# Four residual blocks on one core: the last residual added by an identity matmul and copied by ACT, and the first normalisation made by GpSimd

## The chip, the cores and the metric

The kernel runs on one core of a Trainium2 chip. The metric is device time in microseconds (us) of one execution; before the change the median of 3 runs is 767.77 us (767.4 to 771.08). Engines are called by the names of the profile: PE (TensorE), DVE (VectorE), ACT (ScalarE), POOL (GpSimd) and SP (SyncE, which here only issues DMAs).

## The reference

The input x has 8 samples of 16 channels of 128 x 128 float32 values. Four residual blocks follow, each on a group normalisation (8 groups of 2 channels) of the current x. Cut to what matters:

```
x = x + conv3x3_reflect(_gn(x), sum_n route[n] * w_experts[n]) + bias   # route = softmax(mean(_gn(x)) @ fc_w.T + fc_b)
x = x + conv3x3_depthwise(abs(_gn(x)), weight)                          # zero padding
x = x + box17x17_mean(_gn(x))                                           # zero padding
x = x + L3(_gn(x))

def L3(v):
    nbr = sum of the 8 neighbours of v                                  # zero padding
    h = elu(w1 @ repeat(nbr, 8, axis=1))                                # 64 hidden channels, per pixel
    h = elu(w2 @ h); h = elu(w3 @ h); h = elu(w4 @ h)
    F = w5 @ h                                                          # 64 channels, meaned by fours, * 0.1
    return 16 channels
```

The change touches the first normalisation (`_gn` ahead of the first convolution) of samples 3 to 7, and the addition of L3's result to x.

## The kernel before, in words

All eight samples stay in SBUF (`xs`), 128 partitions (8 image rows by 16 channels) by 2048 elements a sample, and are updated in place. A sample is worked in four chunks, or quarters, of 512 elements a partition, which is one PSUM bank. The four blocks of a sample are run by all engines, each with its own written-out order of instructions and semaphores between them:

- Block 0: normalised rows go to `y0` with one reflected column at either side; DMAs issued by SP copy shifted rows into the windows `win0`; PE multiplies those with the mixed weights (`conv_taps`, banks `pc`), DVE adds the result to x (`evacuate`).
- Block 1: the same with `y1`, `win1`. ACT makes `y1`.
- Block 2: POOL normalises into `y2` (a multiplication and an addition for each chunk), DVE makes running sums along rows (`box_scan` into `box_sum`), PE adds over rows by `box_mat` (`box_band`).
- Block 3: DVE normalises into `y3` (which lies in `box_sum`), POOL adds neighbours (`near_sums`), SP's DMAs stack them (`stacks`), and then come four layers of 64 channels with ELU. The four banks `pz` hold four groups of rows. For each layer PE fills bank after bank (`layer`), ACT makes a relu of the negative part and an exp, and DVE joins both (`join` in `elu`, line 991). The fifth product, `last_layer`, fills the bank `po`, and DVE adds `po` to x (`output`, line 1011).

After a set-up and a prologue, every engine runs rounds t = 1 to 8 (`rounds`; 2 to 4 are a hardware loop). In round t the ELU layers of sample t-1 are the frame: 16 steps, numbered `at` = 4 x quarter + layer, and around them lie block 2 of sample t, blocks 0 (rest), 1 and 3's preparation of samples t and t+1, and the start of sample t+2. The output of quarter p is made behind the first layer (l = 0) of the next quarter. In round 8 (and the first quarter of round 7) two of the four banks are clipped on DVE instead of being put through a relu on ACT (`clips`).

ACT makes the first normalisation of sample t+2 (`normal0`, line 579) at steps 6 to 9, one chunk a step:

```
if at in (6, 7, 8, 9):
    normal0(t + 2, at - 6)
```

POOL's order in a round is: scales of block 1, mixing the weights of sample t+2 (`mix`, `spread`), clearing the edges of `y3` (`edges3`), scales of block 3, neighbour sums, scales of blocks 0 and 2, and `normal2`. SP's order is: store of sample t-2, windows of block 1, windows of block 0, stacks; in round 1 the load of sample 5 stands between the two windows.

Of the kernel before, what the change touches and what calls it, by code (L numbers as in the profile page):

```python
# [21 lines left out]
Q = 4  # L22
# [53 lines left out]
def build(nc, x, w_experts, conv_bias, fc_w, fc_b, w_depth, w1, w2, w3, w4, w5, con_early, con_channel, con_late, out):  # L76
    with ExitStack() as ctx:
        def sb(name, shape, dtype=F32):
            return ctx.enter_context(nc.sbuf_tensor(name, shape, dtype))
# [4 lines left out]
        def sem(name):  # L84
            return ctx.enter_context(nc.semaphore(name))
# [16 lines left out]
        near_sum = sb("near_sum", [P, K, W])  # L102
        stack = [sb(f"stack{m}", [P, K, W]) for m in range(M)]
        box_mat = sb("box_mat", [P, 3, P])

        u = sb("u", [P, M, CH])
# [70 lines left out]
        y3_written = sem("y3_written")  # L178
        y3_edges = sem("y3_edges")
        y2_scaled = sem("y2_scaled")  # L180
        box_rows = sem("box_rows")
        near_pairs_done = sem("near_pairs_done")
        near_pairs_first = sem("near_pairs_first")
# [199 lines left out]
        def _(sp):  # L383
# [14 lines left out]
            def one(t):  # L398
                if has(t - 2):
                    store(t - 2)  # L400
                if has(t + 1):
                    sp.wait_ge(conv_mm[1], 2 * (t + 1))
                    sp.nop(nofuse=True)
                    windows1(sp, t + 1, range(2), True)
                first = isinstance(t, int) and t == 1
                if first:
                    sp.wait_ge(x_loaded, loaded(4))
                    load(5)
                if has(t + 2):
                    sp.wait_ge(conv_mm[0], 2 * (t + 2))  # L410
                    sp.nop(nofuse=True)
                    windows0(sp, t + 2, range(2), True)
                if has(t):
                    stacks(sp, t, 0)
                    stacks(sp, t, 1)
                if first:
                    sp.wait_ge(x_loaded, loaded(5))
                    load(6)
                    sp.wait_ge(x_loaded, loaded(6))
                    load(7)  # L420
# [27 lines left out]
        def _(pool):  # L448
# [39 lines left out]
            def normal2(i, c):  # L488
# [7 lines left out]
                pool.wait_ge(y2_scaled, Q * i + c + 1 - Q)  # L496
                pool.tensor_tensor(rows, rows, two, ALU.add).then_inc(y2_written, 1)

            def edges3(i):

                pool.wait_ge(conv_mm[2], Q * i + Q)
                pool.nop(nofuse=True)
                for at in (0, W + 1):
                    pool.memset(y3[:, :, at:at + 1], 0.0).then_inc(y3_edges, 1)
# [15 lines left out]
            def one(t):  # L520
                if has(t + 1):
                    scales(t + 1, 1)
                if has(t + 2):
                    mix(t + 2)
                    spread(pool, t + 2)
                if has(t):
                    edges3(t)
                    scales(t, 3)
                    for c in range(Q):
                        near_sums(t, c)  # L530
                if has(t + 3):
                    scales(t + 3, 0)
                if has(t + 1):
                    scales(t + 1, 2)
                    for c in range(Q):
                        normal2(t + 1, c)
# [25 lines left out]
        def _(act):  # L562
# [43 lines left out]
            def elu(j, q, l):  # L606
# [20 lines left out]
                else:  # L627
# [3 lines left out]
                        exp(m - 1)  # L631
                    exp(M - 1)

            def one(t):
                first = isinstance(t, int) and t == 1
                for p in range(4):
                    for l in range(LAYERS):
                        at = 4 * p + l
                        elu(t - 1, p, l)
                        if has(t + 1):  # L640
                            if at - first in (4, 5):
                                normal1(t + 1, at - first - 4)
                        if has(t + 2):
                            if at == 5 + first:
                                softmax_exp(t + 2)
                            if at in (6, 7, 8, 9):
                                normal0(t + 2, at - 6)

            for c in range(Q):
                normal0(0, c)  # L650
# [16 lines left out]
            windows1(act, 1, (1,), False)  # L667
            stacks(act, 0, 1)
            rounds(act, one)

        @block.tensor
        def _(pe):
# [83 lines left out]
                    last.then_inc(z_mm, 1)  # L757

            def last_layer(j, q):
                pe.wait_ge(g_written, zn(j, q, LAYERS - 1, M - 1))  # L760

                for m in range(M):
                    last = pe.matmul(po[32 * m:32 * m + 32, :], w5T[:, :], elus(LAYERS - 1)[:, m, :],  # L763
                                     start=True, stop=True)
                last.then_inc(out_mm, 1)

            def one(t):
# [105 lines left out]
        def _(dve):  # L873
# [134 lines left out]
                if l == LAYERS - 1 and not carried(j, q):  # L1008
                    join(l, 3)

            def output(j, q):
                dve.wait_ge(out_mm, Q * j + q + 1)
                dve.tensor_tensor(sample(j, q), po[:, :], sample(j, q), ALU.add).then_inc(out_evac, 1)

            def box_scan(i, c):

                if c == 0:
# [36 lines left out]
            def one(t):  # L1054
                first = isinstance(t, int) and t == 1
                for p in range(4):
                    for l in range(LAYERS):
                        at = 4 * p + l
                        elu(t - 1, p, l)
                        if l == 0 and part_before(t, p):  # L1060
                            output(*part_before(t, p))
                        if has(t + 1):
                            if first and at < 2:
                                evacuate(t + 1, 0, at)
# [97 lines left out]
            for d, side in enumerate(("above", "own", "below")):  # L1162
                last = dve.tensor_copy(box_mat[:, d, :], const(f"box_{side}"))
            last.then_inc(matrices, 1)
            evacuate_pair(0, 0, 0)
            stats_of(0, 1, (0, 2))
            evacuate_pair(0, 0, 1)
# [47 lines left out]
            merge_stats(1, 2)  # L1215
            group_var(1, 2)
            rounds(dve, one)
            output(B - 1, Q - 1)

SETUP_DVE = 6 + 9
# [23 lines left out]
```

## Time and profile before

| | before |
|---|---|
| median of 3 runs | 767.77 us |
| lowest, highest | 767.4, 771.08 us |
| the profiled execution | 776.6 us, span 774.7 us |
| mean granted TensorE clock | 0.945 |
| PE, DVE, ACT, POOL busy | 624.3, 611.5, 563.9, 200.6 us |
| PE weight loads busy | 188.2 us |
| DMA | 85.53 MB in 72865 packets |

The span runs from the first to the last instruction of the profiled execution. Busy time counts the time in which at least one instruction of an engine is in work; instructions of one engine overlap, so that the distance of two starts is often shorter than the duration of one.
### The profile page before, as it was taken

What the parts mean: (1) busy time and instruction counts of PE and PEld (TensorE: products, weight loads), DVE (VectorE), ACT (ScalarE), POOL (GpSimd) and SP (SyncE); (2) the same over time, 40 slices, a digit from 0 to 9 for tenths busy, and PEclk for the clock granted to TensorE, in tenths of its full rate; (3) what the DMA queues carried; (4) which work ended last, traced back from release to release, by engine and by line L of the source; (5) the groups of instructions that cost most, each with busy time, mean ns of one, the idle gap of its engine ahead of it and who ended that gap; (6) DMA issues with size and microseconds to landing.
All of it is one profiled execution on the core that took longest, in us unless ns stands there. A gap on an engine that the chain in (4) does not pass through costs nothing.

```text
span 774.7 us, 13144 instructions
## 1 busy us (share of the span) xinstructions
PE 624.3 (81%) x4142; PEld 188.2 (24%) x4142; DVE 611.5 (79%) x1100; ACT 563.9 (73%) x1081; POOL 200.6 (26%) x291
## 2 busy tenths in 40 slices
PE   0351845899798999899889988999899789889992
PEld 0211211223222222233223322322232223222220
DVE  1352785598959998989988998879887889769993
ACT  0112110689868998899889988998898968898882
POOL 1302024402541235213521353125300630230000
PEclk9985886899989999999999999999999999999996
DMA  5759499407985739254834574455640560065002
GB/s 98 139 91 178 101 189 211 73 14 146 170 192 97 173 88 206 66 112 107 183 87 109 110 164 107 109 112 132 141 109 3 125 146 1 2 146 125 1 1 54
DMA packets 72865, 85.53 MB, mean 110 GB/s; under 512 B 8674, under 2 KB 58354, under 8 KB 72818
## 3 DMA queue, kind: packets, MB, share of 16 engines
q1 hardware_dynamic: 68096, 78.58, 47.6%
q10 hardware_dynamic: 4722, 6.34, 4.5%
q8 instruction: 26, 0.43, 0.2%
q14 instruction: 21, 0.17, 0.1%
HBM read 9.14 MB, written 8.39 MB: 23 GB/s over the span
## 4 chain that ended last, share of the span: by engine, by line
PE 36%; DVE 22%; ACT 17%; DMA 8%; issue 8%; SPq 6%; POOL 1%; ACTq 1%; DVEq 0%; POOLq 0%
PE pz L756 19%; PE pc L702 8%; ACT u L610 7%; DVE g L991 6%; ACT u L618 6%; PE pc L733 6%; DMA win<-y 5%; DVE u L987 3%; ACT u L615 2%; DVE bn L923 2%; DVE box_sum L1024 2%; DMA xs<-in_x_dram 2%; DVE xs L974 2%; PE po L763 2%; DMA stack<-near_sum 2%
## 5 line engine op out<-in xcount | busy, mean ns | idle before, releaser
L610 ACT ACTIVATE u<-pz 128x512 f32<-128x512 f32 x472 | 275.4, 603 | 93.3 <-PE pz L756 92.7
L756 PE MATMUL pz<-g,wT 64*64 64x512 f32 x1536 | 296.7, 614 | 18.7 <-DVE g L991 15.1
L991 DVE SCALAR_TENSOR_TENSOR g<-u,pz 128x512 f32<-128x512 f32 x384 | 250.3, 681 | 62.1 <-ACT u L618 58.7
L618 ACT ACTIVATE u<-u 128x512 f32<-128x512 f32 x472 | 289.6, 643 | 1.3
L756 PEld LDWEIGHTS pz<-g,wT 64*64 64x64 f32 x1536 | 80.5, 132 | 212.2 <-issue 210.4
L733 PE MATMUL pc<-win,t 64*32 64x512 f32 x1392 | 98.0, 667 | 27.0 <-DMA win<-y 16.0
L702 PE MATMUL pc<-box_sum,box_mat 128*128 128x512 f32 x180 | 90.9, 621 | 12.3 <-DVE box_sum L1024 12.3
L923 DVE BATCH_NORM_STATS2 bn<-xs 128x6 f32<-128x512 f32 (+1 forms) x128 | 82.8, 682 | 22.0 <-DMA xs<-in_x_dram 20.2
L468 POOL TENSOR_TENSOR stat<-stat,con 128x1 f32<-128x1 f32 x32 | 22.5, 704 | 272.9 <-DVE stat L943 272.9
L991 DVE SCALAR_TENSOR_TENSOR g_last<-u,pz 128x512 f32<-128x512 f32 x128 | 82.5, 680 | 9.1 <-ACT u L618 7.1
L756 PE MATMUL pz<-stack,wT 64*64 64x512 f32 x512 | 81.7, 620 | 9.5 <-DMA stack<-near_sum 4.2
L678 PE MATMUL psm<-stat,con 128*128 128x2 f32 x64 | 12.8, 270 | 56.9 <-DVE stat L931 53.6
L598 ACT ACTIVATE y<-xs,stat 128x1024 f32<-128x1024 f32 (+1 forms) x16 | 19.9, 1258 | 43.7 <-POOL stat L471 43.7
L702 PEld LDWEIGHTS pc<-box_sum,box_mat 128*128 128x128 f32 x180 | 29.9, 188 | 72.7 <-issue 46.1
L733 PEld LDWEIGHTS pc<-win,t 64*32 64x32 f32 x1392 | 24.2, 114 | 93.2 <-issue 93.2
L1024 DVE TENSOR_TENSOR_SCAN box_sum<-y 128x580 f32<-128x580 f32 x32 | 43.1, 1355 | 1.4 <-DMA stack<-near_sum 1.4
L514 POOL TENSOR_TENSOR near_sum<-box_sum 128x512 f32<-128x512 f32 x30 | 31.8, 1059 | 39.5 <-DVE box_sum L1031 39.5
L584 ACT ACTIVATE y<-xs,stat 128x512 f32<-128x512 f32 (+1 forms) x32 | 26.3, 839 | 19.2 <-POOL stat L471 10.1
L518 POOL TENSOR_TENSOR near_sum<-near_sum,box_sum 128x512 f32<-128x512 f32 x30 | 37.7, 1258 | 4.3 <-DVE near_sum L1052 2.0
L756 PEld LDWEIGHTS pz<-stack,wT 64*64 64x64 f32 x512 | 23.5, 134 | 60.3 <-issue 58.1
L763 PE MATMUL po<-g_last,w5T 128*32 128x512 f32 x256 | 35.0, 619 | 2.8 <-DVE g_last L991 2.8
L615 ACT ACTIVATE u<-u 128x512 f32<-128x512 f32 x40 | 25.2, 629 | 12.2 <-DVE u L987 12.2
(87 smaller groups left out, 366.6 us busy)
## 6 DMA issues: line engine op xcount, KB each, us to landing
stack<-near_sum SPq DMA_DIRECT2D x90, 192.0 KB, 4.0
win<-y SPq DMA_DIRECT2D x56, 260.0 KB, 4.2
win<-y SPq DMA_DIRECT2D x56, 195.0 KB, 4.3
out_dram<-xs SPq DMA_DIRECT2D x8, 1024.0 KB
stack<-box_sum SPq DMA_DIRECT2D x60, 128.0 KB, 3.8
xs<-in_x_dram SPq DMA_DIRECT2D x7, 1024.0 KB
stack<-near_sum SPq DMA_DIRECT2D x30, 128.0 KB, 3.4
win<-y ACTq DMA_DIRECT2D x8, 260.0 KB, 8.2
```

The costliest lines, as they stand in the source:

```text
L514: pool.tensor_tensor(o, y[:, :, 0:W], y[:, :, 1:W + 1], ALU.add).then_inc(near_pairs_done, 1)
L518: pool.tensor_tensor(o, o, y[:, :, 2:W + 2], ALU.add).then_inc(near_rows, 1)
L610: act.activation(u[:, m, :], pz[:, m, :], ACT.Relu, scale=-1.0, bias=0.0).then_inc(relu_done, 1)
L615: act.activation(u[:, m, :], u[:, m, :], ACT.Exp).then_inc(exp_done, 1)
L618: act.activation(u[:, m, :], u[:, m, :], ACT.Exp, scale=-1.0).then_inc(exp_done, 1)
L702: mm = pe.matmul(chunk_bank(i, c), box_mat[:, d, :], box_sum[:, c * KB + d:(c + 1) * KB + d, RAD:RAD + W], start=d == 0, stop=d == 2)
L733: last = pe.matmul(pair_banks(i, k, n)[2 * C * m:2 * C * m + 2 * C, h, :], mat[rows, kw, :], blocks(win[m // 2], n + 2 * h)[rows, :, kw:kw ...
L756: last = pe.matmul(pz[to, m, :], wT[rows, l, rows], src, start=True, stop=True)
L763: last = pe.matmul(po[32 * m:32 * m + 32, :], w5T[:, :], elus(LAYERS - 1)[:, m, :], start=True, stop=True)
L923: dve.bn_stats(bn[k][:, c, :], sample(i, c)).then_inc(stat_step[k], 1)
L991: dve.scalar_tensor_tensor(out=elus(l)[:, m, :], in0=u[:, m, :], scalar=-1.0, in1=pz[:, m, :], op0=ALU.add, op1=ALU.max).then_inc(g_writte ...
L1024: dve.tensor_tensor_scan(own_rows(box_sum, c).rearrange("p k w -> p (k w)"), y2[:, c * n + BOX:(c + 1) * n + BOX], y2[:, c * n:(c + 1) * n ...
```

## The change

Three things are altered.

- `last_layer` first multiplies the chunk of x itself with a 128 x 128 identity (`same`, copied from the constants once by DVE) into `po`, and the four products with `w5T` are then added in the bank. ACT copies the bank over the chunk of x; DVE's addition is gone. PE's identity matmul waits for ACT's previous copy.
- `normal0` of samples 3 to 7 goes from ACT's steps 6 to 9 to POOL, ahead of `mix`, as a multiplication and an addition for each chunk and two column copies for each pair of chunks; POOL waits first for all four scans of sample t (`box_rows`). Samples 0 to 2 stay with ACT in the prologue.
- On SP, in round 1, the load of sample 5 stands behind the windows of block 0 instead of ahead of them.

```diff
@@ sync, one(t)
-                if first:
-                    sp.wait_ge(x_loaded, loaded(4))
-                    load(5)
                 if has(t + 2):
                     sp.wait_ge(conv_mm[0], 2 * (t + 2))
                     sp.nop(nofuse=True)
                     windows0(sp, t + 2, range(2), True)
+                if first:
+                    sp.wait_ge(x_loaded, loaded(4))
+                    load(5)
@@ gpsimd
+            def normal0(i, c):
+
+                if c == 0:
+                    pool.wait_ge(norm_step[0], i * NORM + NORM)
+                    pool.wait_ge(win0_in, WIN0 * i)
+                rows = blocks(y0, c)[:, :, 1:W + 1]
+                one, two = (st[0][:, n:n + 1].unsqueeze(2).to_broadcast([P, KB, W]) for n in range(2))
+                pool.tensor_tensor(rows, sample(i, c).rearrange("p (k w) -> p k w", w=W), one, ALU.mult).then_inc(y0_scaled, 1)
+                pool.wait_ge(y0_scaled, Q * i + c + 1 - 3 * Q)
+                pool.tensor_tensor(rows, rows, two, ALU.add).then_inc(y0_written, 1)
+                if c % 2:
+                    half = slice((c - 1) * KB, (c + 1) * KB)
+                    pool.wait_ge(y0_written, Y0 * i + 2 * c)
+                    pool.nop(nofuse=True)
+                    pool.tensor_copy(y0[:, half, 0:1], y0[:, half, 2:3]).then_inc(y0_written, 1)
+                    pool.tensor_copy(y0[:, half, W + 1:W + 2], y0[:, half, W - 1:W]).then_inc(y0_written, 1)
...
                 if has(t + 2):
+                    pool.wait_ge(box_rows, Q * t + Q)
+                    for c in range(Q):
+                        normal0(t + 2, c)
                     mix(t + 2)
@@ scalar
+            def output(j, q):
+                act.wait_ge(out_mm, Q * j + q + 1)
+                act.copy(sample(j, q), po[:, :]).then_inc(out_evac, 1)
...
                         elu(t - 1, p, l)
+                        if l == 0 and part_before(t, p):
+                            output(*part_before(t, p))
...
-                            if at in (6, 7, 8, 9):
-                                normal0(t + 2, at - 6)
@@ tensor
             def last_layer(j, q):
+                if isinstance(j, int) and j == 0 and q == 0:
+                    pe.wait_ge(matrices, 2)
+                else:
+                    pe.wait_ge(out_evac, Q * j + q)
+                pe.nop(nofuse=True)
+                pe.matmul(po[:, :], same[:, :], sample(j, q), start=True, stop=False)
                 pe.wait_ge(g_written, zn(j, q, LAYERS - 1, M - 1))
-
+                pe.nop(nofuse=True)
                 for m in range(M):
                     last = pe.matmul(po[32 * m:32 * m + 32, :], w5T[:, :], elus(LAYERS - 1)[:, m, :],
-                                     start=True, stop=True)
+                                     start=False, stop=True)
@@ vector
-            def output(j, q):
-                dve.wait_ge(out_mm, Q * j + q + 1)
-                dve.tensor_tensor(sample(j, q), po[:, :], sample(j, q), ALU.add).then_inc(out_evac, 1)
...
-                        if l == 0 and part_before(t, p):
-                            output(*part_before(t, p))
...
+            dve.tensor_copy(same[:, :], const("ident")).then_inc(matrices, 1)
```

In DVE's and ACT's lists the output behind the last round goes from one to the other as well.

POOL in the loop of rounds 2 to 4, from the scales of block 1 on, before (`wmix` are the mixed weights, `stat` the statistics and scales):

```order
L468 TENSOR_TENSOR stat<-stat,con 128x1
L469 REGISTER_ALU
L471 TENSOR_SCALAR stat<-stat 128x1
L477 ISA
L479 TENSOR_SCALAR wmix<-wc,route 128x144
```

The same place of the changed kernel, down to the first mixing (`y` is `y0` here, `xs` the samples):

```order
L473 TENSOR_SCALAR stat<-stat 128x1
L543 ISA
L504 ISA
L505 REGISTER_ALU
L508 ISA
L508 TENSOR_TENSOR y<-xs,stat 128x4x128
L509 ISA
L510 TENSOR_TENSOR y<-y,stat 128x4x128
L508 ISA
L508 TENSOR_TENSOR y<-xs,stat 128x4x128
L509 REGISTER_ALU
L510 TENSOR_TENSOR y<-y,stat 128x4x128
```

Two chunks and two column copies, and the same again, now stand between POOL's scales of block 1 and its mixing; L543 is the wait for the scans.

PE around a quarter's first layer in the loop, before (`po` is the output bank, `stack` the layer's input, L702 a box band, L756 the layers):

```order
L756 MATMUL pz<-stack,wT 64x512 x2
L763 MATMUL po<-g_last,w5T 32x512 x4
L702 MATMUL pc<-box_sum,box_mat 128x512
L752 REGISTER_ALU
L756 MATMUL pz<-g,wT 64x512 x2
```

The same place of the changed kernel (L783 are the layers, L792 the identity, L796 the last layer, L729 the band):

```order
L783 MATMUL pz<-stack,wT 64x512 x2
L790 REGISTER_ALU
L792 ISA
L792 MATMUL po<-xs,same 128x512
L796 MATMUL po<-g_last,w5T 32x512 x4
L729 MATMUL pc<-box_sum,box_mat 128x512
L779 REGISTER_ALU
L783 MATMUL pz<-g,wT 64x512 x2
```

One 128 x 128 by 512 matmul, with a wait and a register for its address, has come between the first layer of a quarter and the second.

## Rows read from the trace of the kernel before

**Rows 1.** Windows of rounds 4, 6 and 8: busy us of each engine.
```profile
core 0: us, PE busy (x) PEld busy (x) DVE busy (x) ACT busy (x) POOL busy (x), PEclk, DMA share, GB/s
386.70:466.00 79.30, 73.23 (x520) 22.24 (x516) 72.22 (x129) 71.52 (x140) 26.15 (x37) 1.00 0.55 120
...
544.70:620.10 75.40, 67.79 (x432) 20.27 (x426) 64.73 (x110) 68.40 (x131) 20.34 (x24) 1.00 0.40 91
...
695.30:760.30 65.00, 59.29 (x282) 13.40 (x274) 61.68 (x99) 56.17 (x96) 0.00 (x0) 1.00 0.19 43
```

**Rows 2.** Waits over the span: engine, line, awaited, us, times, longest.
```profile
ACT u L610 <- PE pz L756: 92.7, 54, 32.9
```

**Rows 3.** Timeline of ACT, round 6: start, us, instruction, idle before.
```profile
574.43 1.12 ACT L610 ACTIVATE u<-pz 128x512 f32<-128x512 f32 x2
...
578.45 1.20 ACT L610 ACTIVATE u<-pz 128x512 f32<-128x512 f32 x2
...
583.60 1.08 ACT L610 ACTIVATE u<-pz 128x512 f32<-128x512 f32 x2 [0.90 <-PE pz L756]
```

**Rows 4.** Timeline of PE, round 6, the same steps.
```profile
580.55 1.99 PE L702 MATMUL pc<-box_sum,box_mat 128*128 128x512 f32 x4
582.48 2.31 PE L756 MATMUL pz<-stack,wT 64*64 64x512 f32 x16
584.72 1.06 PE L763 MATMUL po<-g_last,w5T 128*32 128x512 f32 x8
585.72 1.13 PE L702 MATMUL pc<-box_sum,box_mat 128*128 128x512 f32 x2
586.78 1.95 PE L756 MATMUL pz<-g,wT 64*64 64x512 f32 x10
```

**Rows 5.** Timelines of SP, PE and ACT in round 1; the last is round 3.
```profile
182.62 0.71 SPq L385 DMA_DIRECT2D xs<-in_x_dram  x1
183.44 10.46 SPq L339 DMA_DIRECT2D win<-y  x5
...
199.23 1.23 SPq L347 DMA_DIRECT2D win<-y  x2
...
212.45 3.67 PE L733 MATMUL pc<-win,t 64*32 64x512 f32 x32 [3.98 <-DMA win<-y]
...
218.07 1.09 ACT L610 ACTIVATE u<-pz 128x512 f32<-128x512 f32 x2 [7.37 <-PE pz L756]
...
376.60 1.09 ACT L610 ACTIVATE u<-pz 128x512 f32<-128x512 f32 x2 [1.43 <-PE pz L756]
```

**Rows 6.** Timelines of DVE (the last scan) and POOL in round 4.
```profile
416.73 1.36 DVE L1024 TENSOR_TENSOR_SCAN box_sum<-y 128x580 f32<-128x580 f32 x1
...
423.92 0.65 POOL L479 TENSOR_SCALAR wmix<-wc,route 128x144 f32<-128x144 f32 x1 [15.51 <-DVE route L963]
...
437.02 0.57 POOL L468 TENSOR_TENSOR stat<-stat,con 128x1 f32<-128x1 f32 x1 [7.09 <-DVE stat L943]
```

**Rows 7.** POOL's normal2: one line's durations (min, median, max), and a group.
```profile
L495 POOL TENSOR_TENSOR y<-xs,stat x28: 1039/1042/1043, 136.1 to 624.1; 128x512 f32<-128x512 f32 x28
...
L497 POOL TENSOR_TENSOR y<-y,stat 128x512 f32<-128x512 f32 x28 | 29.3, 1045 | 2.2
```

**Rows 8.** Timeline of ACT in round 4, the first normalised chunk.
```profile
420.66 0.88 ACT L584 ACTIVATE y<-xs,stat 128x512 f32 x1
421.36 1.15 ACT L610 ACTIVATE u<-pz 128x512 f32<-128x512 f32 x2
```

**Rows 9.** Timelines of PE and DVE in round 8, and PE's end.
```profile
713.32 1.06 PE L763 MATMUL po<-g_last,w5T 128*32 128x512 f32 x8
714.32 2.25 PE L756 MATMUL pz<-g,wT 64*64 64x512 f32 x12
...
715.26 0.68 DVE L1013 TENSOR_TENSOR xs<-po,xs 128x512 f32<-128x512 f32 x1
715.86 0.68 DVE L991 SCALAR_TENSOR_TENSOR g<-u,pz 128x512 f32<-128x512 f32 x1
...
761.05 1.94 PE L763 MATMUL po<-g_last,w5T 128*32 128x512 f32 x8 [2.80 <-DVE g_last L991]
```

More of the change, by code:

```diff
@@ L104, in build @@
         box_mat = sb("box_mat", [P, 3, P])
+        same = sb("same", [P, P])
         u = sb("u", [P, M, CH])
@@ L180, in build @@
         y2_scaled = sem("y2_scaled")
+        y0_scaled = sem("y0_scaled")
         box_rows = sem("box_rows")
@@ L669, in _ @@
             rounds(act, one)
+            output(B - 1, Q - 1)
         @block.tensor
@@ L1217, in _ @@
             rounds(dve, one)
-            output(B - 1, Q - 1)
 SETUP_DVE = 6 + 9
```

## The prediction

> **What bounds the kernel now.** I read first the busy table cut by round, then the waits, and then the steps of single rounds on ACT, PE and DVE. A round is sixteen steps (four quarters of four layers). In round 4, a middle one, no engine is full: PE is busy 73.2 of 79.3 us, DVE 72.2, ACT 71.5, POOL 26.2 [rows 1]. ACT's relu waits for PE 54 times, 92.7 us in all, the longest 32.9 ahead of round 1 [rows 2]. So a round is a chain that goes through ACT, DVE and PE in turn, and two rules give the start of the next step:
>
> - ACT's rule: a bare step lasts 4.0 us (574.43 to 578.45, eight activations 0.5 apart) [rows 3], and everything else ACT runs is added.
> - PE's rule: the last join of a step lets PE finish the fourth bank of the next layer; then PE does what it has been given behind that layer, and only then the first bank of the layer after it, which ACT's first relu waits for. So a step's start is tied to the start two steps earlier. In round 6, where ACT has no normalisation to make, two such starts lie 583.60 - 574.43 = 9.17 apart with two box bands in between that hold PE from 580.55 to 582.48, 1.93 us [rows 3, 4]. So two steps take at least 7.24 us plus what PE has behind the middle layer; ACT alone needs 8.0 for two. PE can hide 0.76 us per layer, and more where ACT is given other work.
>
> Carried through the sixteen steps of a middle round with DVE's joins 0.60 apart, these rules give 79.4 us for the 79.3 of [rows 1], so I trust them for differences.
>
> **The stall of round 1.** At step 13 ACT stands for 7.37 us; the same place in round 3 has 1.43 [rows 5]. PE waited there for window DMAs (3.98 us) and its next 32 matmuls took 3.67 us. The cause is on SP: the load of sample 5 (1 MB) went out at 182.62, and the first five window copies behind it took 10.46 us to issue; the last pair went out at 199.23 [rows 5]. The change puts these copies ahead of the load. POOL writes y0 earlier than ACT did: it starts behind the last scan, which in round 4 ends at 416.73 + 1.36 = 418.09 [rows 6]; four chunks of 1.042 + 1.045 = 2.09 us [rows 7] make 8.4, with edges and semaphores some 9.3, done at about 427.4, whereas ACT only starts its first chunk at 420.66 and does one per step [rows 8]. So the fourteen copies can go out from 182.6 at some 0.7 us each (1.23 for the last two) and end near 192.5, eight us before the last pair of today; the stall falls to the usual one: 7.37 - 1.43 = **5.9 us gained**. Bounds: nothing gained (the load now runs into the stack copies that follow) and 7.4.
>
> **What POOL pays.** The mix and spread of the same sample, which start at 423.92 today, start at about 427.5 and end some 5.5 us later with the edge memsets, 433; the next thing POOL is waited for is the scale at 437.02, before which it sits 7.09 us [rows 6]. Four us of cover stay, so I price it at nothing; without the cover each us late would be a us on the third scale and the stacks behind it. The added wait on box_rows also holds back those memsets, but nothing that is due earlier than 437.
>
> One doubt is whether POOL's eight instructions and DVE hold each other up. Of POOL's 28 multiplications of the other normalisation, made beside DVE's joins, additions and statistics, the shortest takes 1039 and the longest 1043 ns [rows 7], so they don't; normal0 will run beside the same kinds of DVE work, since the scans are over by then.
>
> **The steps with l = 0.** Four times a round PE gets an identity matmul, ACT a copy, and DVE loses an addition.
> - Identity: 128x128 weights and 512 columns, the shape of one box band. The single band behind the last layer occupies PE from 585.72 to 586.78, 1.06 us [rows 4]. Half of the pair of bands is 0.97. I take 1.06; the ends are 0.5, if part of it falls into PE's own gaps, and 2.0, if its weights or its register address can't be prepared under the layer before.
> - Copy: 0.50, an eighth of a bare step, which is what a relu from such a bank costs [rows 3]; the ends are 0.40 and the 0.70 (420.66 to 421.36) that a normalised chunk takes [rows 8].
> - Addition gone: DVE's own pitch, 715.26 to 715.86, 0.60 [rows 9].
> - normal0 gone from ACT in rounds 1 to 5: 0.70 and, with edges, about 1.1, twice each, 3.6 us a round [rows 8]. What this is worth is seen in round 6, which has none: ACT then waits 0.90 for PE at the very next step [rows 3]. Most of the 3.6 turns into waiting for PE.
>
> Behind an l = 0 layer PE has the last layer (1.00: 584.72 to 585.72) and a band or tap (1.06) [rows 4]: the two-step minimum is 7.24 + 2.06 = 9.30 today and 10.36 with the identity. Carried through a middle round: first quarter +0.4 (the step behind the identity starts 0.9 later, the DVE addition gives 0.5 back, and the rest delays the scans that PE waits for); second -0.2 (ACT bound: +0.5 copy, -0.7 normal0); third +0.1 (+0.9, normal0 gone); fourth -0.4 (+0.8, but two convolution taps that wait for evacuations on DVE start 0.6 earlier each). Sum -0.1: **-0.4 for rounds 2 to 5**.
>
> Round 6 (75.4 us) has no normal0 to lose and round 7 no convolutions [rows 1]: there the identity and the copy are only partly absorbed by the next step's wait, by the same rules **+0.9 each**.
>
> Round 8 (65.0 us, 4.06 a step [rows 1]) is another chain: two banks are clipped on DVE, and clip, exp and join follow one another on DVE and ACT. The next layer starts on PE at 714.32, exactly when the last layer (from 713.32) lets it [rows 9], and it sets the next relu. The identity moves that by 1.06; DVE's addition, 0.60 ahead of the next step's join, gives some 0.4 back, and 0.2 of the rest is free on ACT. That leaves 0.45 a quarter, four times: **+1.8**, with ends 0 (all in gaps) and 4.2 (nothing given back).
>
> At the end the identity lies in PE's wait of 2.80 us for the last join [rows 9], and ACT's copy replaces DVE's 0.68 us addition: nothing. Behind that wait the eight passes of the last layer take 1.94 us against 1.06 in round 6 [rows 4, 9]. The Trainium skill (TensorE: Matmul & The Clock Gate, What's actually happening) says that the array's clock is cut to half when it has been idle and released by activity. By that rule an identity inside the wait could keep the clock up and the last layer be 0.9 shorter, and the sum below would be -3.6; the trace alone gives nothing, since PE still stands for some 1.7 us, and the sum goes by that. The extra DVE copy of the identity (128x128) comes once, in the set-up, where DVE waits for the first convolution: nothing, at most 0.2.
>
> **Sum.** -5.9 - 0.4 + 0.9 + 0.9 + 1.8 = -2.7 against the profiled execution, 776.6 us (span 774.7). That run is 1.1% above the median of 767.77, so I scale: 773.9 / 776.6 x 767.77 = **765.1 us**, 0.35% faster.
>
> **Rivals.**
> - ACT was the bound after all, and all its saving shows. Rounds 1 to 5 then gain 3.6 - 4 x 0.5 = 1.6 each, 8.0, rounds 6 and 7 lose 2.0 each for the copies, round 8 gains the 1.6 of DVE, beside the stall's 5.9: 11.5 us, 756.4. For it: ACT's steps 4 to 9 have no idle time in round 4. Against: the 0.90 of round 6 [rows 3]. Chance 0.12.
> - The stall moves: the load, now behind the windows, is still on the queues when the stack copies of sample 1 are issued, and the first layer of round 2 waits for those. Then the 5.9 is lost: +3.2, 770.9. For it: the load kept SP's queue slow for 10.46 us [rows 5], and the stack copies are the next on that queue. Chance 0.12.
> - Slower: the identity costs about 2.0 us instead of 1.06, since its moving operand comes from an address in a register and its full-width weights may not load under the layer before. Its place is behind every l = 0 layer, where PE's rule is the later one; each 0.1 above 1.06 costs by the rules 0.3 to 0.4 a round over seven rounds. At 1.2 the gain is gone; at 2.0 the total is about +19, 786.6. Against: bands of the same shape stand at 1.06 and their banks and rows vary too. Chance 0.10, of it 0.03 with a cost so small above 1.2 that it can't be told from no change.
> - The forecast: chance 0.66, its own range 761.5 to 768.5.
>
> **How the numbers follow.** About 0.5% (3.8 us) is what a measurement of this kernel can tell from no change, so faster is below 763.9 and slower above 771.6. The forecast gives 0.22 faster and 0.44 same; the first rival 0.12 faster; the moved stall 0.07 same and 0.05 slower; the dear identity 0.03 same and 0.07 slower. That is faster 0.34, same 0.54, slower 0.12. The range 760.0 to 770.8 holds the forecast whole, most of the moved stall and a cheap identity (0.5 instead of 1.06, some 5 us less).
>
> **What would show it.** Right: in round 1 PE has no DMA wait near step 13, and SP's five copies issue in about 4 us; the round is near 82 us; rounds 2 to 5 stay within 0.5 us of 79.3; rounds 6 and 7 grow by about 1 and round 8 by about 2; ACT's waits for PE come behind l = 0 layers. Wrong: an identity pair that holds PE more than 1.2 us, a stack wait at the start of round 2, POOL's third scale later than DVE's statistics by more than today, or middle rounds shorter by over 1 us.

## The result: 772.75 us, 0.4% slower than before

The changed kernel took 772.75 us (median of 20 executions, 769.45 to 781.46), the kernel before 769.9 (20 executions, 766.07 to 774.05). The execution of 781.46 is over 1.5% slower than the fastest and is left out of the ratio, which is 1.0039, 95% interval 1.0023 to 1.0054. The forecast was 765.1, with a range of 760.0 to 770.8: the time lies outside it, and on the other side of no change. The chance of 0.54 for "within 0.5%" holds the ratio; the time and the direction were wrong.

The two profiled executions alone would have told the opposite: the span fell from 774.7 to 771.5 us, 3.2 less, where the sum said 2.7 less. So the comparison of the two profiles and that of the timed executions disagree by 6 us, and most of what follows looks for these.

**The profile after.** A round's length is taken here from ACT's first activation of the round to that of the next. First the windows of rounds 4, 6 and 8, which answer [rows 1]:

```profile
381.10:460.60 79.50, 75.01 (x529) 22.54 (x524) 70.71 (x126) 70.48 (x136) 34.97 (x49) 1.00 0.53 119
539.40:615.90 76.50, 69.99 (x438) 20.30 (x430) 62.56 (x106) 69.89 (x134) 19.84 (x23) 1.00 0.42 96
690.60:757.90 67.30, 59.06 (x292) 14.70 (x290) 60.72 (x98) 58.27 (x100) 0.00 (x0) 1.00 0.19 43
```

Round 4 is 79.5 long (79.3 before), round 6 76.5 (75.4), round 8 67.3 (65.0). DVE does 1.5 us less in round 4, POOL 8.8 more, ACT 1.0 less. ACT waits for PE as long in sum as before [rows 2], but more often, 70 times and not 54:

```profile
ACT u L632 <- PE pz L783: 92.4, 70, 32.1
```

The place of the stall in round 1 (timelines of SP, PE and ACT; answers [rows 5]):

```profile
183.32 3.73 SPq L341 DMA_DIRECT2D win<-y  x5
...
187.73 3.69 SPq L341 DMA_DIRECT2D win<-y  x5
...
193.44 0.71 SPq L387 DMA_DIRECT2D xs<-in_x_dram  x1
...
207.97 1.95 PE L760 MATMUL pc<-win,t 64*32 64x512 f32 x32
...
220.00 1.95 PE L783 MATMUL pz<-stack,wT 64*64 64x512 f32 x16
...
211.01 1.19 ACT L632 ACTIVATE u<-pz 128x512 f32<-128x512 f32 x2
```

Each five copies issue in 3.7 us, the load leaves at 193.44, and neither the 32 window matmuls nor the stack layer behind them, nor ACT, has a wait in its brackets. The step did what it was meant to do.

GpSimd in round 4 (timelines of DVE and POOL, and below them POOL's groups: busy, mean ns, idle before; answers [rows 6] and [rows 7]):

```profile
412.07 1.36 DVE L1053 TENSOR_TENSOR_SCAN box_sum<-y 128x580 f32<-128x580 f32 x1
...
413.78 1.04 POOL L508 TENSOR_TENSOR y<-xs,stat 128x512 f32<-128x512 f32 x1 [10.26 <-DVE box_sum L1053]
...
423.20 0.65 POOL L481 TENSOR_SCALAR wmix<-wc,route 128x144 f32<-128x144 f32 x1
...
432.84 0.57 POOL L470 TENSOR_TENSOR stat<-stat,con 128x1 f32<-128x1 f32 x1 [4.27 <-DVE stat L976]
```

```profile
L508 POOL TENSOR_TENSOR y<-xs,stat 128x512 f32<-128x512 f32 x20 | 20.8, 1041 | 46.1 <-DVE box_sum L1053 46.1
L510 POOL TENSOR_TENSOR y<-y,stat 128x512 f32<-128x512 f32 x20 | 20.8, 1040 | 1.6
```

The normalisation starts behind the last scan and holds POOL 9.4 us (413.78 to 423.20; 9.3 was expected); the third scale still waits 4.27 us for DVE: that cover is left, four us were expected, and the delay that was priced at nothing costs nothing there.

The identity, in round 8 and at the end (timelines of PE and ACT; answers [rows 4] and [rows 9]):

```profile
709.22 1.12 PE L792 MATMUL po<-xs,same 128*128 128x512 f32 x2
710.27 1.06 PE L796 MATMUL po<-g_last,w5T 128*32 128x512 f32 x8
711.27 1.99 PE L783 MATMUL pz<-g,wT 64*64 64x512 f32 x16
714.51 7.63 PE L783 MATMUL pz<-g,wT 64*64 64x512 f32 x32 [1.26 <-DVE g L1024]
...
711.40 0.59 ACT L658 COPY xs<-po 128x512 f32<-128x512 f32 x1
712.39 0.60 ACT L632 ACTIVATE u<-pz 128x512 f32<-128x512 f32 x1 [0.40 <-PE pz L783]
...
758.69 1.07 PE L796 MATMUL po<-g_last,w5T 128*32 128x512 f32 x8 [1.83 <-DVE g_last L1024]
```

The two records of the identity hold PE for 1.05 us (709.22 to 710.27), as the band it was priced by. The copy takes 0.59. What the price of 0.45 a quarter left out is the row at 714.51: PE then also waits 1.26 us for a join. Its exponential came late because ACT's relu, at 712.39, stood 0.40 for the layer that the identity had put off; the copy had ended by then, so it was not the copy that held ACT. In the kernel before, PE ran 34 matmuls without a wait from the same place on (timeline of PE, before):

```profile
714.32 8.18 PE L756 MATMUL pz<-g,wT 64*64 64x512 f32 x34
```

### The profile page after: what moved, and what is told of

Read it like the earlier page. It is cut to its first block, busy times and chain, and to the rows that moved or that the text cites. A ratio compares the mean times of both kernels' runs of the same rounds, so it can differ in the third digit from the quotient of the medians.

```text
span 771.5 us, 13403 instructions
## 1 busy us (share of the span) xinstructions
PE 627.5 (81%) x4206; PEld 190.7 (25%) x4206; DVE 598.9 (78%) x1069; ACT 564.2 (73%) x1073; POOL 243.8 (32%) x351
## 4 chain that ended last, share of the span: by engine, by line
PE 51%; DVE 15%; ACT 12%; issue 7%; DMA 7%; SPq 5%; POOL 1%; ACTq 1%; DVEq 0%; POOLq 0%
PE pz L783 26%; PE pc L760 8%; PE pc L729 7%; ACT u L632 5%; DVE g L1024 5%; ACT u L640 4%; DMA win<-y 4%; PE po L792 4%; PE po L796 4%; DVE bn L956 3%; DVE box_sum L1053 3%; SPq L356 2%; DMA xs<-in_x_dram 2%; DVE xs L1007 1%; SPq L376 1%
## 5 line engine op out<-in xcount | busy, mean ns | idle before, releaser
L640 ACT ACTIVATE u<-u 128x512 f32<-128x512 f32 x472 | 287.8, 639 | 1.3
L783 PE MATMUL pz<-g,wT 64*64 64x512 f32 x1536 | 268.4, 606 | 20.4 <-DVE g L1024 18.7
L783 PEld LDWEIGHTS pz<-g,wT 64*64 64x64 f32 x1536 | 73.0, 131 | 191.9 <-issue 189.9
L760 PE MATMUL pc<-win,t 64*32 64x512 f32 x1392 | 93.5, 639 | 23.3 <-DMA win<-y 15.3
L729 PE MATMUL pc<-box_sum,box_mat 128*128 128x512 f32 x180 | 90.9, 621 | 11.0 <-DVE box_sum L1053 11.0
L783 PE MATMUL pz<-stack,wT 64*64 64x512 f32 x512 | 86.2, 621 | 7.7 <-issue 4.2
L729 PEld LDWEIGHTS pc<-box_sum,box_mat 128*128 128x128 f32 x180 | 29.9, 188 | 71.4 <-issue 46.4
L783 PEld LDWEIGHTS pz<-stack,wT 64*64 64x64 f32 x512 | 24.8, 134 | 61.8 <-issue 59.4
L792 PE MATMUL po<-xs,same 128*128 128x512 f32 (+1 forms) x64 | 36.0, 645 | 0.0
L796 PE MATMUL po<-g_last,w5T 128*32 128x512 f32 x256 | 34.1, 604 | 1.8 <-DVE g_last L1024 1.8
L508 POOL TENSOR_TENSOR y<-xs,stat 128x512 f32<-128x512 f32 x20 | 20.8, 1041 | 46.1 <-DVE box_sum L1053 46.1
```

What stands on the lines that cost most here:

```text
L640: act.activation(u[:, m, :], u[:, m, :], ACT.Exp, scale=-1.0).then_inc(exp_done, 1)
L729: mm = pe.matmul(chunk_bank(i, c), box_mat[:, d, :], box_sum[:, c * KB + d:(c + 1) * KB + d, RAD:RAD + W], start=d == 0, stop=d == 2)
L760: last = pe.matmul(pair_banks(i, k, n)[2 * C * m:2 * C * m + 2 * C, h, :], mat[rows, kw, :], blocks(win[m // 2], n + 2 * h)[rows, :, kw:kw ...
L783: last = pe.matmul(pz[to, m, :], wT[rows, l, rows], src, start=True, stop=True)
L792: pe.matmul(po[:, :], same[:, :], sample(j, q), start=True, stop=False)
```

## The experiments

Two theories stood against each other. Theory 1: the stall of round 1 differs from one execution to the next, the profiled execution of before had a large one, and a typical one has little to gain. Theory 2: the stall is in every execution of before, and something in the changed kernel that its profile didn't show takes the gain back. Beside them: which of the three parts (the residual on PE and ACT, the normalisation on POOL, the load's place) costs and which gives.

### The kernel before, five more times

No edit.

> The kernel before, unchanged, for a second profiled execution and a second set of times. Theory 1 (the profiled execution of before, 776.6 us, was untypical and the 7.37 us stall of round 1 varies from one execution to the next): ratio 1.000, and the new profile has a span of 766 to 771 us with a stall before ACT's first middle layer of step 13 of round 1 of under 4 us; round 1 lasts 81 to 85 us, not 88.08. Theory 2 (the stall stands in every execution of before, and something else in the typical execution of after takes back 6 to 9 us): the new profile has the stall at 6.5 to 8 us, round 1 at 87 to 89 us, and a span near 774.

> The kernel before, unchanged, a third time. Theory 1 (the wait of round 1 differs between executions: 7.37 and 4.4 us of ACT's idle time so far): ratio 0.998 to 1.003, and another size of the wait, 1 to 7 us, with SyncE's five window copies again at 10 us. Theory 2 (the wait is always there at 4 us or more): 4 to 8 us.

> The kernel before, one more profiled execution for the size of the round 1 wait (ACT idle behind step 13: 7.37, 4.31 and 5.03 us so far). Theory 1: another value between 2 and 8 us, and the rounds 2 to 8 again within 1.5 us of 546 us.

> The kernel before, a fifth profiled execution, for the size of the wait. Theory 1: a wait of 1 to 5 us (7.37, 4.31, 5.03 and 2.85 so far) and a time that rises with it: near 767 with 2 to 3 us, near 772 with 5. Theory 2: 4 us or more.

> The kernel before, a sixth profiled execution, for the same. Theory 1: 1 to 5 us. Theory 2: 4 us or more.

Measured, timed: 1.003 (1.0002 to 1.0057) and 0.9998 (0.9964 to 1.0031) of before. The first of these reads an unchanged kernel as 0.3% slower, so no single ratio below is trusted closer than that. The six profiled executions, in us (the wait is the one that ACT's first activation behind step 13 of round 1 has for PE):

```
execution            1st    2nd    3rd    4th    5th    6th    mean
time               776.6  774.01 771.14 767.05 764.49 764.63
span               774.7  772.1  769.2  765.1  762.5  762.7   767.7
ahead of round 1   139.92 143.01 137.17 138.54 136.88 136.97  138.75
ACT's wait           7.37   4.31   5.03   2.85   2.06   1.50    3.85
round 1             88.08  84.03  85.52  82.62  81.79  81.22   83.88
round 2 to the end 546.7  545.1  546.5  543.9  543.8  544.5   545.1
```

In the sixth, PE has no wait for the window copies at all (timeline of PE, then of SP):

```profile
205.28 1.95 PE L733 MATMUL pc<-win,t 64*32 64x512 f32 x32 [0.72 <-DVE xs L977]
...
178.44 0.71 SPq L385 DMA_DIRECT2D xs<-in_x_dram  x1
179.47 9.60 SPq L339 DMA_DIRECT2D win<-y  x5
```

The slow issue behind the load is there in every execution (9.60 to 10.46 us for the five copies); whether the last copies land late enough for PE to wait is what differs. With the usual 1.50 taken off, the stall was 5.9, 2.8, 3.5, 1.4, 0.6 and 0 us: 2.4 in the mean. Theory 1 missed some of its sizes: the second execution (4.31 us and a span of 772.1, where it said under 4 and 766 to 771), the fourth (543.9 us from round 2 on, where it said at least 544.5) and the fifth (764.49 us, where it said near 767). That the size of the wait differs holds; theory 2 rested on 4 us or more each time, and three of six are below. The first execution, the one that the prediction was read from, is the slowest of the six and has the longest stall. The six together are a fair sample: the mean of their times is 769.65 us, the median of the 20 timed executions 769.9.

### The changed kernel, three more times

No edit.

> The changed kernel a second time. Theory 1 (its profiled execution, round 1 at 80.6 us, is typical, and the time is 550.4 us from round 2 on as against 545 to 547 before): ratio 0.999 to 1.003, a profile with round 1 at 80 to 82 us. Theory 2 (a wait that the first profile did not show takes back the gain in most executions): 1.003 to 1.006, round 1 at 83 us or more, or a later round 2 us longer than in the first profile.

> The changed kernel, a third profiled execution. Theory 1 (the order of the copies takes the wait away in every execution, and the rest costs 4 to 5 us from round 2 on): round 1 at 80.3 to 80.9 us with no wait of TensorE for window or stack copies, rounds 2 to the end at 549 to 551 us, whatever the set-up ahead of round 1 takes (137 to 143 us in the executions so far). Theory 2 (a wait that the first two profiles missed): round 1 over 82 us.

> The changed kernel, a fourth profiled execution, for the same: by theory 1 round 1 at 80.3 to 80.9 us and 549 to 551 us from round 2 on, by theory 2 round 1 over 82 us.

Measured: 1.0045 (1.0024 to 1.0066) of before, so the loss is there twice. By the time that is theory 2's range; the profiles are theory 1's. In the four profiles (first run's and these), ACT's wait behind step 13 is 0 each time, round 1 lasts 80.63, 80.49, 81.74 and 80.61 us, round 2 to the end 550.4, 549.3, 550.2 and 549.8 (mean 549.9), and what is ahead of round 1 140.50, 140.95, 139.02 and 137.40 (mean 139.5). The 81.74 missed the 80.3 to 80.9: it lies in the first step of the round, not at the load. The mean span is 770.25.

Mean against mean: 139.5 - 138.75 = +0.7 ahead of round 1 (inside the scatter), 80.87 - 83.88 = -3.0 in round 1, 549.9 - 545.1 = +4.8 from round 2 on, together +2.5 us, or 0.33%. That lies within both timed intervals. No hidden wait is needed, none is seen in four profiles, and theory 2 falls.

### The load's place alone, and taken out of the change

The first kernel makes this edit to before, the second takes it back in the changed kernel.

```diff
-                if first:
-                    sp.wait_ge(x_loaded, loaded(4))
-                    load(5)
                 if has(t + 2):
                     sp.wait_ge(conv_mm[0], 2 * (t + 2))
                     sp.nop(nofuse=True)
                     windows0(sp, t + 2, range(2), True)
+                if first:
+                    sp.wait_ge(x_loaded, loaded(4))
+                    load(5)
```

> Before, with SyncE's sixth load of round 1 put behind the next part's window copies, and nothing else. Theory 1 (stall mostly absent in typical executions): ratio 0.997 to 1.001, since there is hardly anything to gain. Theory 2 (stall in every execution): ratio 0.990 to 0.993 (5.5 to 7.4 us of 770 gone). Both: the profiled execution has no DMA wait of PE near step 13 of round 1, and round 1 lasts 80 to 82 us.

> The changed kernel with the sixth load of round 1 put back ahead of the window copies. Theory 1: 1.003 to 1.007 of before, that is within 0.3% of the changed kernel, because the order of the load matters little in a typical execution. Theory 2: 1.010 to 1.014 of before, as the stall of 6 to 7 us returns on top of the 3 us of the rest.

Measured: 1.0023 (0.9994 to 1.0053) for before with the load behind, and 1.0086 (1.0049 to 1.0122) for the changed kernel with the load ahead again, between the two expectations: 776.71 us against 772.75 and 772.49 for the changed kernel. So the same reorder gives nothing in one kernel, and taking it back costs 3.2 to 3.6 us in the other by the ratios (1.0086 against 1.0045 and 1.0039, the intervals just meet); the profile of that run has ACT's wait again, 3.74 us. In the first, round 1 lasts 85.7 us where both theories said 80 to 82. Its timelines of SP and PE say why:

```profile
191.72 3.60 SPq L339 DMA_DIRECT2D win<-y  x5
...
197.26 0.71 SPq L385 DMA_DIRECT2D xs<-in_x_dram  x1
203.94 0.55 SPq L373 DMA_DIRECT2D stack<-near_sum  x1
...
207.75 1.95 PE L733 MATMUL pc<-win,t 64*32 64x512 f32 x32 [0.72 <-DVE xs L977]
...
222.66 2.89 PE L756 MATMUL pz<-stack,wT 64*64 64x512 f32 x16 [3.05 <-DMA stack<-near_sum]
```

The window wait is gone, and a stack wait of 3.05 us stands in its place: that is the rival "the stall moves". The second five copies wait for y0's second half, which ACT writes late (they start at 191.72, 53.7 us into the round, against 187.73, 47.2 us into it, in the changed kernel), so the load leaves only 6.7 us ahead of the stack copies, and 10.4 in the changed kernel, where POOL has the half ready. The prediction placed the copies by POOL's earlier rows, but its rival of the moved stall does not say that it hangs on them. Two of the runs below agree: 6.6 us and a stack wait without POOL, 11.5 us and none with it.

### The residual part alone, and with the reorder

```diff
+                pe.matmul(po[:, :], same[:, :], sample(j, q), start=True, stop=False)
...
+                act.copy(sample(j, q), po[:, :]).then_inc(out_evac, 1)
...
-                dve.tensor_tensor(sample(j, q), po[:, :], sample(j, q), ALU.add).then_inc(out_evac, 1)
```

> Before with the identity matmul, ACT's copy out of the bank and the copy of the identity matrix, without the GpSimd normalisation and without the reorder of the load. Theory 1: the residual part carries the loss: 1.004 to 1.008 of before (3 to 6 us; 32 identity matmuls at 1.06 us and 32 copies of 0.50 us on ACT against 32 additions of 0.60 us on DVE, of which about a tenth shows). Rival (the GpSimd normalisation carries the loss, by waits for the second part's rows): 0.998 to 1.002 here.

> Before with the residual part and the load behind the window copies, the normalisation left on ScalarE. Both theories: 1.008 to 1.012, as for the residual part alone, since ScalarE's late second half of the normalisation holds back the second five window copies and with them the load, which then delays the stack copies: a wait of 2 to 5 us at the last step of round 1. If the load's place were a gain by itself: 1.003 to 1.006.

Measured: 1.0106 (1.0073 to 1.0140) and 1.0128 (1.0082 to 1.0173). Both lie above what was expected: the residual part carries the loss, and more than all of it. Round 4 of the first (window) and the stack wait of the second (timeline of PE, round 1):

```profile
382.60:462.70 80.10, 75.76 (x528) 22.70 (x524) 70.80 (x125) 73.37 (x144) 26.13 (x37) 1.00 0.53 118
```

```profile
227.01 3.72 PE L764 MATMUL pz<-stack,wT 64*64 64x512 f32 x16 [6.09 <-DMA stack<-near_sum]
```

In the first, middle rounds grow to 80.1 us and round 2 to the end to 552.6, 7.5 above before. In the second, the reorder without POOL again brings the stack wait, 6.09 us here, where 2 to 5 were expected.

### The normalisation on GpSimd alone, and with the reorder

```diff
+                    for c in range(Q):
+                        normal0(t + 2, c)      # pool, behind the last scan
...
-                            if at in (6, 7, 8, 9):
-                                normal0(t + 2, at - 6)      # act
```

> Before with the first normalisation on GpSimd behind the last scan, and nothing else. Theory A (the three parts add up: the residual part costs 6 to 7 us, the normalisation gives 2 us, the load's place 3.6 us): 0.996 to 0.999, with rounds 3 to 5 at 78.6 to 79.0 us and the wait of round 1 still there. Theory B (the normalisation only gives back what the residual's copies put on ScalarE): 0.999 to 1.003, rounds 3 to 5 at 79.3.

> Before with the normalisation on GpSimd and the load behind the window copies; the addition of the residual stays on VectorE. Theory A: 0.990 to 0.994 (some 5 to 7 us less than before: no wait for windows or stack copies in round 1, 0.5 us less in each middle round), faster than both kernels. Theory B: 0.994 to 0.997, the wait of round 1 alone.

Measured: 0.9967 (0.9940 to 0.9994) and 0.9962 (0.9937 to 0.9987). Theory A's size for the first was right; the second gave less than its 0.990 to 0.994: the two times, 766.88 and 767.04 us, can't be told apart. In the profile of the first, ACT's wait behind step 13 is 2.61 us, so that only 1.1 of stall was there to take. This 0 and the 3.2 to 3.6 of the changed kernel are each a difference of two ratios with intervals of 0.2 to 0.4%, and both agree with a stall of 2.4 in the mean. A middle round of the second (window of round 4):

```profile
383.80:462.70 78.90, 72.68 (x520) 22.06 (x516) 72.47 (x129) 68.60 (x132) 34.91 (x49) 1.00 0.54 121
```

Round 2 to the end is 542.3 and 543.3 us, 2 to 3 under the mean of before, and rounds 3 and 4 take 78.9, where all six executions of before have 79.3 to 79.4. In time both kernels beat before by hardly more than the 0.3% that an unchanged kernel showed, so that rests on the rounds as much as on the ratios; they beat the changed kernel clearly. As far as these runs show, the change is worth having without its residual part.

### The residual part taken apart

```diff
-                pe.matmul(po[:, :], same[:, :], sample(j, q), start=True, stop=False)
...
-                                     start=False, stop=True)
+                                     start=True, stop=True)
```

> The changed kernel without the 32 identity matmuls, so that the residual is not added; ScalarE's copy, the waits and all else stay. If the identity's 1.06 us on TensorE is the price of the residual part: 0.994 to 0.998 of before, that is 4 to 6 us under the changed kernel, with round 8 back at 65 to 66 us and rounds 3 to 5 at 79.0 to 79.3. If ScalarE's copy is the price: 1.001 to 1.004, round 8 at 66.8 or more.

```diff
-                act.copy(sample(j, q), po[:, :]).then_inc(out_evac, 1)
+                dve.tensor_copy(sample(j, q), po[:, :]).then_inc(out_evac, 1)
```

> The changed kernel with the identity matmul kept and VectorE copying the bank in place of ScalarE. If the identity is the price: within 0.2% of the changed kernel or above it (1.002 to 1.006 of before). If ScalarE's copy is the price: 0.996 to 0.999, with round 8 at 65 to 66 us.

Measured: 0.9912 (0.9890 to 0.9935) without the identity, lower than foreseen (this kernel leaves out the addition of the residual, so it prices the identity and is no alternative), and 1.0066 (1.0042 to 1.0090) with the copy on DVE. Windows of rounds 4 and 8, and PE in round 8, without the identity:

```profile
376.75:455.17 78.42, 73.94 (x520) 21.82 (x516) 70.61 (x125) 70.40 (x137) 34.92 (x49) 1.00 0.55 121
681.33:745.70 64.37, 57.58 (x282) 13.62 (x280) 59.97 (x96) 57.32 (x100) 0.00 (x0) 1.00 0.20 45
```

```profile
699.20 1.06 PE L795 MATMUL po<-g_last,w5T 128*32 128x512 f32 x8
700.19 3.04 PE L783 MATMUL pz<-g,wT 64*64 64x512 f32 x16
703.80 7.62 PE L783 MATMUL pz<-g,wT 64*64 64x512 f32 x32 [0.56 <-DVE g L1023]
```

The identity is the price: 1.0045 - 0.9912 = 1.3%, 10.2 us for 32 of them, 0.32 us each, 30% of the 1.06 for which one holds PE. A middle round gives back 1.1 us, round 8 3.1 (from 67.4), and PE's wait for the join in the same quarter falls from 1.26 to 0.56. The copy is on the better engine: on DVE the middle rounds are 80.1 and not 79.5 in the profiles, while the timed intervals of the two overlap.

So from round 2 on, in profiled executions: 545.1 before (mean of six); 542.8 with the normalisation on POOL (mean of the two); 540.0 with ACT's copy in the place of DVE's addition too (one execution); 549.9 with the identity (mean of four). In steps that is -2.3, -2.8 and +9.9. The residual part alone, +7.5, is close to the last two steps together, +7.1.

### The load far behind

```diff
                 if first:
+                    sp.wait_ge(x_loaded, loaded(4))
+                    load(5)                    # behind the stack copies
                     sp.wait_ge(x_loaded, loaded(5))
                     load(6)
```

> Before with the sixth load put behind the stack copies of round 1, where neither window nor stack copies stand behind it in the queue until round 2. The profile must show no DMA wait at steps 13 and 15 of round 1, and round 1 at 79.5 to 81 us. Theory 1 (the wait of round 1 is small in a typical execution of before, 2 to 3 us): 0.996 to 0.998. Theory 2 (it is 5 to 7 us in a typical execution): 0.991 to 0.994.

> The normalisation on GpSimd with the sixth load behind the stack copies, the addition left on VectorE. Theory 1: 0.993 to 0.997, that is no more than 0.2% under the normalisation on GpSimd alone (0.9967). Theory 2: 0.988 to 0.992.

Measured: 1.0180 (1.0157 to 1.0203) and 1.0122 (1.0098 to 1.0146): both theories missed. The timelines of SP and PE of the first:

```profile
226.14 25.13 SPq L385 DMA_DIRECT2D xs<-in_x_dram  x3
251.70 6.34 SPq L395 DMA_DIRECT2D out_dram<-xs  x1
258.32 9.33 SPq L354 DMA_DIRECT2D win<-y  x1
...
280.31 3.67 PE L732 MATMUL pc<-win,t 64*32 64x512 f32 x32 [12.75 <-DMA win<-y]
```

Three loads in a row, each waiting for the one before, hold SP to 251.3; the store and then the windows of round 2 come late, and round 2 lasts 94.0 us in place of 79.5. The timed ratio therefore prices another wait than the one that it was to price. What can be read is round 1: ACT's wait is 1.50, as in the sixth execution of before, and the round 81.5 us, 2.4 under the mean of before, the size of theory 1. The second run shows the same, with 94.9 us for round 2.

## Why the prediction was wrong

1. **The failed step** is the term of round 1: "the stall falls to the usual one: 7.37 - 1.43 = 5.9 us gained". Cause, place and cure were right: the load ahead of the window copies, SP's slow five copies, no DMA wait afterwards, and POOL finishing early enough. Most of the signs that were named for a right forecast came true in the first profile for the same reason (no wait near step 13, copies in 3.7 us, round 8 longer by 2.3): they tell whether the stall goes, not how much of it a typical execution has. The size was wrong: 5.9 is the largest of six executions, whose mean is 2.4 and whose smallest is 0. Round 1 as a whole (the other parts work there too) gained 3.0 in the mean.
2. **The scaling hid it.** The profiled execution of before stood 8.8 us above the median, and 5.5 above the slowest of the three times. The prediction multiplied by 767.77 / 776.6, which treats the excess as spread over the run. Of the 7.0 us by which its span exceeds the mean of six, 4.2 lie in round 1, most of them in the very stall that was to be taken away. So a gain of 5.9 was taken off a median of executions that have 2.4 of it in the mean. The starting figure was off too: 767.77 is a median of three, 769.9 that of 20, and these 2.1 us are part of the 7.7 by which the time missed 765.1.
3. **The identity** was priced right as an instruction (1.06 expected, 1.05 measured) and somewhat too low on the path. Expected against measured (means of six and of four executions): rounds 2 to 5 -0.4 against +0.7 (316.8 to 317.55), round 6 +0.9 against +1.4, round 7 +0.9 against +0.7, round 8 +1.8 against +2.2, end 0 against -0.3: +3.2 against +4.8. Round 8 missed the join's wait on the row at 714.51.
4. **Cover on POOL**, four us expected, 4.27 measured: right. The identity's copy in the set-up: no difference that the scatter ahead of round 1 lets one see.
5. **The last layer** is no sure term. It took 1.94, 1.94, 1.07, 1.07, 1.93 and 1.93 us in the executions of before, each behind a wait of 2.80, and 1.07, 1.06, 1.93 and 1.06 in those of the changed kernel, behind 1.83 or 1.84 and an identity ahead of that. The windows show a granted clock of 0.50 (1.2 GHz) in a long one of before and 0.52 in the long one of the changed kernel, and 1.00 (2.4 GHz) in short ones of both. By the rule that the prediction took from the Trainium skill (TensorE: Matmul & The Clock Gate, What's actually happening), that activity releases the clock, the last layer could be 0.9 us shorter behind an identity. The end got 0.3 in the mean: both levels occur with the identity and without it, so it did not settle the level by itself.
6. **The rivals.** ACT as the bound: against it, ACT's waits became more, and middle rounds of the changed kernel did not shrink (79.5 against 79.3). The moved stall: no in this change, yes where POOL does not normalise. The dear identity: no, 1.05. What came instead is the forecast itself with a term of 5.9 that a typical execution does not have: with 2.4 in its place the same sum is -2.4 - 0.4 + 0.9 + 0.9 + 1.8 = +0.8, no change, and the 1.6 us of point 3 make it 2.4.

## What to carry to other kernels

When the profiled execution is slower than the timed ones, first find in it what the others can't have; a gain that removes just that must not be counted in full. A transfer's wait in one trace is one draw, so bound it from zero and put the typical value near what the median leaves room for. And work given to an engine that is not full can still cost time where that engine stands in a chain: here about a third of its duration. Test the parts alone, because here one part paid and another took it back.

## What the runs showed that was not expected

- The set-up ahead of round 1 takes 136.9 to 143.0 us in six executions of before and 137.4 to 141.0 in four of the changed kernel. With round 1 (81.2 to 88.1) it makes up most of the spread of before (span 762.5 to 774.7).
- A DMA wait can cost twice. Behind waits of 3.98 and 2.56 us the 32 window matmuls ran 3.67 and 3.65 us; behind 3.53, 2.07 and 1.29 us they ran 1.95. Over just these matmuls the granted clock is 0.50 (1.2 GHz) in the first execution, behind 3.98, 0.53 in the third, behind 2.56, and 1.00 (2.4 GHz) in the second, behind 3.53. The length of the wait alone does not order them. So of the stall of 5.9 us only 3.3 were the longer wait for the copies (3.98 against the 0.72 that PE stands there in the sixth); the rest came from slow matmuls behind it.
- Round 7 of before takes 71.7 to 75.9 us in six executions, with a wait for stack copies at its end of 0.47 us in the shortest and 2.60 in the first; the changed kernel's takes 74.4 to 74.75. What steadies it was not tried.
